# A Mamba scan on one Trainium2 core: C rows for five GpSimd products instead of three, brought by broadcast transfers

## The reference, cut to what matters

```python
h = relu(adj @ layernorm(x) @ gcn_w + gcn_b); h = layernorm(h) * ln_g + ln_b
xc, z = split(h @ w_in); u = silu(causal_conv4(xc))
dbc = u @ w_xp
dt = softplus(dbc[:, :8] @ w_dt + b_dt)
B, C = dbc[:, 8:24], dbc[:, 24:40]
hst = exp(dt*A) * hst + dt*B*u          # a recurrence over the 8192 tokens, for each channel and state
y = (sum over the 16 states of hst * C) + u * D_skip
x = x + (y * silu(z)) @ w_out
```

## Time and profile before

| | us |
|---|---|
| median of three runs | 1697.73 (1697.00 to 1698.45) |
| the profiled execution | 1698.79 |
| its span, first to last instruction | 1696.9 |
| steps 4 to 15, from ScalarE's copy at the head of step 4 to that of step 16 | 294.43 to 1246.9 |

### The profile page before, as it was taken

One profiled execution on the slowest core, in us unless ns is written; L12 is line 12 of the kernel. 1 busy time (PEld: TensorE's weight loads), 2 busy tenths in 40 slices (PEclk: granted clock), 3 DMA queues, 4 the chain that ended last, 5 costly groups with the idle time before them and its releaser, 6 DMA issues. The chain is left out here.

```text
span 1696.9 us, 21136 instructions
## 1 busy us (share of the span) xinstructions
PE 1556.1 (92%) x5282; PEld 791.8 (47%) x5282; DVE 1482.2 (87%) x1687; ACT 1005.5 (59%) x2093; POOL 1041.3 (61%) x471
## 2 busy tenths in 40 slices
PE   6999999999999999999999999999977677999994
PEld 2444344444444434343444444444422225999993
DVE  8416999999999999999999999999996995557998
ACT  2244666667575757576666667575757554555552
POOL 4024788887878778878788787878885651001221
PEclk9999999999999999999999999999988899999997
DMA  8976665757566666665665757566610202000002
GB/s 311 343 253 236 229 213 196 255 169 272 197 241 224 215 242 205 235 214 213 224 229 187 257 171 269 203 237 230 209 47 0 94 6 106 0 0 1 0 0 99
DMA packets 52073, 298.31 MB, mean 176 GB/s; under 512 B 5522, under 2 KB 5522, under 8 KB 19092
## 3 DMA queue, kind: packets, MB, share of 16 engines
q1 hardware_dynamic: 49680, 293.30, 48.8%
q10 hardware_dynamic: 2308, 4.20, 0.6%
HBM read 285.68 MB, written 11.80 MB: 175 GB/s over the span
## 5 line engine op out<-in xcount | busy, mean ns | idle before, releaser
L509 PE MATMUL bank<-ring,xh 128*128 128x512 f32 x2048 | 953.1, 593 | 15.5 <-DVE xh L989 15.0
L890 POOL TENSOR_TENSOR work<-work 128x1024 f32<-128x1024 f32 x210 | 516.6, 2460 | 238.3 <-DVE work L1081 232.0
L1123 DVE TENSOR_TENSOR_SCAN work<-bank,hstate,work 128x512 f32<-128x512 f32 x512 | 627.2, 1266 | 2.7 <-ACT bank L760 1.3
L509 PEld LDWEIGHTS bank<-ring,xh 128*128 128x128 f32 x2048 | 388.4, 190 | 458.3 <-issue 422.3
L760 ACT ACTIVATE bank<-work,a_neg 128x512 f32<-128x512 f32 x512 | 345.6, 688 | 306.2 <-DVE work L1123 305.9
L1073 DVE TENSOR_TENSOR work<-work,bank 128x1024 f32<-128x1024 f32 x256 | 309.5, 1214 | 60.0 <-PE bank L446 46.3
L446 PE MATMUL bank<-bc_parts,sel 96*128 96x512 bf16 x512 | 192.9, 385 | 33.3 <-DVE work L1081 25.8
L1081 DVE TENSOR_TENSOR work<-work,bank 128x1024 f32<-128x1024 f32 x182 | 216.2, 1194 | 0.0
L441 PE MATMUL bank<-work,w_sb 128*128 128x512 f32 (+2 forms) x352 | 183.5, 618 | 25.4 <-ACT work L676 11.2
L951 POOL TENSOR_TENSOR work<-work 128x256 f32 x32 | 28.5, 891 | 235.9 <-ACT work L797 235.9
L853 POOL TENSOR_TENSOR work<-work 128x1024 f32<-128x1024 f32 x48 | 113.3, 2361 | 79.9 <-ACT work L658 79.7
(11 more groups left out here) (148 smaller groups left out, 1581.4 us busy)
## 6 DMA issues: line engine op xcount, KB each, us to landing
ring<-adj_t SPq DMA_DIRECT2D x256, 1024.0 KB, 4.8
xh<-x_rows SPq DMA_DIRECT2D x16, 256.0 KB, 6.7
work<-x_t SPq DMA_DIRECT2D x16, 256.0 KB, 4.8
x_scratch<-work ACTq DMA_DIRECT2D x16, 256.0 KB, 5.4
work<-x_scratch SPq DMA_DIRECT2D x1, 4096.0 KB, 13.6
out_t<-work SPq DMA_DIRECT2D x16, 256.0 KB, 2.7
xl_scratch<-work SPq DMA_DIRECT2D x13, 256.0 KB, 2.2
ring<-xl_scratch SPq DMA_DIRECT2D x1, 3328.0 KB, 13.1
```

The costliest lines, as they stand in the source:

```text
L509: last = nc.tensor.matmul(mixed[:, :], xn[:, j, :], a, start=(j == 0), stop=(j == BLK - 1))
L890: nc.gpsimd.tensor_tensor(out=acc, in0=hc[0] if n == 1 else acc, in1=hc[n % 2], op=ALU.add).then_inc(y_added, 1)
L1123: nc.vector.tensor_tensor_scan(hb[s % 2][:, h, :], da[h], dbu[s % 2][:, h, :], hstate[:, HV * s + h:HV * s + h + 1], ALU.mult, ALU.add).th ...
```

## The change

`POOL_HC` becomes (1, 3, 8, 10, 14). For these five states TensorE's spread of the C row and ScalarE's copy are left out in all steps but the draining ones. Instead, in slot 9 of each step ScalarE stores rows 16 to 31 of `dbc` (the f32 values of C, 32 KB) to a new scratch tensor `c_dram`, and in the next step issues five loads (`load_c`), each of which reads one row of 512 values into all 128 partitions (256 KB), into one of two buffers: for states 1, 3, 8, 10 and 14 in slots 0, 2, 6, 8 and 12. The second buffer `c_two` takes the place of `bias_rows`, so the biases are now loaded at the start of step 16, after GpSimd's last product that reads a row there, and `fold_bias` moves behind slot 0 of that step. TensorE's waits for a free `c_bank` now count VectorE's products only.

```diff
-POOL_HC = (3, 8, 10)
+POOL_HC = (1, 3, 8, 10, 14)
+C_LOAD = {0: 1, 2: 3, 6: 8, 8: 10, 12: 14}
...
+def c_spreads(cs, n):
+
+    if isinstance(cs, int) and cs >= NC - 2:
+        return (DS - len(POOL_HC)) * (NC - 2) + DS * (cs - (NC - 2)) + n + 1
+    return hc_count(cs, n, False)
...
+    c_dram = nc.dram_tensor("c_scratch", (NC, DS, CH), F32, kind="Internal").ap()
...
-        bias_rows = sb("bias_rows", [2, 4 * D])
+        c_two = sb("c_two", [P, CH])
+        bias_rows = c_two[0:2, :]
...
-        c_one = carve(CH)
+        c_rows = [carve(CH), c_two[:, :]]
...
             def step(k, par, adj, pre, scan, post):
-                if isinstance(k, int) and k == NC:
-                    fold_bias()
...
                 def spread_c(n):
-                    if drains(k) and (cs > NC - 2 or n >= 1):
-                        pe.wait_ge(c_copied, hc_count(cs, n - 1, True))
-                    elif n >= 2 and n - 2 in POOL_HC:
-                        pe.wait_ge(c_copied, hc_count(cs, n - 2, True))
-                    else:
-                        wait_hc(pe, cs, n - 2)
+                    if drains(k):
+                        if cs == NC - 2 and n == 0:
+                            pe.wait_ge(hc_done, hc_count(cs - 1, DS - 1, False))
+                        else:
+                            pe.wait_ge(c_copied, DS * (cs - (NC - 2)) + n)
+                    elif n in POOL_HC:
+                        return
+                    elif n >= 2:
+                        wait(pe, hc_done, hc_count(cs, n - 2, False))
+                    elif not (isinstance(cs, int) and cs == 0):
+                        pe.wait_ge(hc_done, hc_count(cs - 1, DS + n - 2, False))
...
                 for s in range(16):
+                    if isinstance(k, int) and k == NC and s == 1:
+                        fold_bias()
...
-            act.dma_start(bias_rows[:, :], lstm_bias).then_inc(bias_loaded, 16)
...
+                if isinstance(k, int) and k == NC:
+                    act.wait_ge(pool_hc_done, len(POOL_HC) * (NC - 2))
+                    act.dma_start(bias_rows, lstm_bias).then_inc(bias_loaded, 16)
...
                     if s == 9:
                         written("dbc")
+                        wait(act, c_stored, 16 * (k - 1))
                         nc.scalar.activation(dbc[0:XPW, :], shared[0:XPW, :], ACT.Copy).then_inc(shared_read, 1)
                         act.wait_ge(shared_read, shared_index("dbc", k, pre, post) + 1)
+                        act.dma_start(c_dram[k - 1], dbc[DS:2 * DS, :]).then_inc(c_stored, 16)
...
+                def load_c(n):
+
+                    i = POOL_HC.index(n)
+                    b = (par + i) % 2
+                    act.wait_ge(c_stored, 16 * (cs + 1))
+                    wait(act, pool_hc_done, hc_count(cs, n, True) - 2)
+                    act.dma_start(c_rows[b], c_dram[cs, n:n + 1, :].broadcast_to([P, CH])).then_inc(c_row_in[b], 16)
...
                 for s in range(16):
-                    if scan and s >= 1 and (drains(k) or s - 1 in POOL_HC):
+                    if scan and drains(k) and s >= 1:
                         copy_c(s - 1)
...
+                    if scan and not drains(k) and s in C_LOAD:
+                        load_c(C_LOAD[s])
...
                 def make_hc(n):
-                    pool.wait_ge(c_copied, hc_count(cs, n, True))
+                    if drains(k):
+                        pool.wait_ge(c_copied, DS * (cs - (NC - 2)) + n + 1)
+                        c = c_sb[n % 2]
+                    else:
+                        i = POOL_HC.index(n)
+                        b = (par + i) % 2
+                        pool.wait_ge(c_row_in[b], 8 * (len(POOL_HC) * cs + (i - b)) + 16)
+                        c = c_rows[b]
...
                 def make_hc(n):
-                    dve.wait_ge(c_ready, DS * cs + n + 1)
+                    dve.wait_ge(c_ready, c_spreads(cs, n))
```

More of the change, by code:

```diff
@@ L265, in build @@
         xt_in = [sem(f"xt_in{i}") for i in range(2)]
+        c_row_in = [sem(f"c_row_in{i}") for i in range(2)]
+        c_stored = sem("c_stored")
         row_sum, row_mean, row_centred, row_sq = sems("row_sum row_mean row_centred row_sq")
@@ L394, in fold_bias @@
                 nc.tensor.matmul(mixed[:, :], less_first[:, :], W("w_ih"), start=True, stop=False)
-                nc.tensor.matmul(mixed[:, :], first_row[:, :], bias_rows[:, :], start=False, stop=True).then_inc(folded, 1)
+                nc.tensor.matmul(mixed[:, :], first_row[:, :], bias_rows, start=False, stop=True).then_inc(folded, 1)
             def step(k, par, adj, pre, scan, post):
-                if isinstance(k, int) and k == NC:
-                    fold_bias()
                 if isinstance(k, int) and k == 1:
@@ L727, in copy_c @@
                 def copy_c(n):
-                    act.wait_ge(c_ready, DS * cs + n + 1)
-                    if drains(k):
-                        act.wait_ge(adj_used, PIECES * NC)
-                        wait_hc(act, cs, n - 2)
-                        dest = c_sb[n % 2]
-                    else:
-                        wait(act, pool_hc_done, hc_count(cs, n, True) - 1)
-                        dest = c_one
-                    nc.scalar.activation(dest, c_bank[0 if drains(k) else n % 2][:, :], ACT.Copy).then_inc(c_copied, 1)
+                    act.wait_ge(c_ready, c_spreads(cs, n))
+                    act.wait_ge(adj_used, PIECES * NC)
+                    wait_hc(act, cs, n - 2)
+                    nc.scalar.activation(c_sb[n % 2], c_bank[0][:, :], ACT.Copy).then_inc(c_copied, 1)
+                def load_c(n):
[4 more added lines that the diff above has]
+                    act.dma_start(c_rows[b], c_dram[cs, n:n + 1, :].broadcast_to([P, CH])).then_inc(c_row_in[b], 16)
                 def save_state(c, n):
@@ L903, in make_hc @@
                         wait(pool, y_added, (DS - 1) * cs + (n - 1))
-                    c = c_sb[n % 2] if drains(k) else c_one
                     nc.gpsimd.tensor_tensor(out=hc[n % 2], in0=hb[n % 2], in1=c.unsqueeze(1).broadcast_to([P, HV, CH]),
```

## The result

The changed kernel takes 1754.35 us (median of 4 runs, 1752.59 to 1755.11) against 1698.09 for the kernel before beside it (4 runs). The ratio is 1.0325, 95% interval 1.0305 to 1.0345. The change was forecast slower by 1.3% and is slower by 3.3%, above the top of the range. The profiled execution took 1755.01 us, its span is 1753.1: 56.2 us more than before where I had summed 22.7.

The account below looks back on a forecast made before the run. Each step was bound by two legs: dtu to dbu 7 through adj piece 2 and TensorE, then to the next dtu through GpSimd. 19.6 - 1.5 + 4.6 = +22.7 us gave 1720.4 us; eight-in-ten range 1701 to 1730.

Parts of the forecast that it names:

- the bound: A loop step has two legs: dtu to dbu 7 through adj piece 2 and TensorE, then to the next dtu through GpSimd.
- the first half of the mechanism: Product 14 on GpSimd ahead of `make_xl` makes the xl store and adj piece 2 2.52 us later; TensorE waits.
- the term for twelve steps: Steps 4 to 15: xc1 and dbu 7 later by 1.29 us (five even steps) or 1.88 (seven others), +19.6 us.
- there are five pairs of adj products of 1.72: TensorE's work from piece 2 to xc1, with small products and xc0, priced at 10.12 us in all.
- Steps 2 and 3: No ring wait there; product 1 and c1, c3 shorten leg one: -1.5 us, between 0 and -2.2.
- Step 16: Start of step 16: biases load only after product 14 of step 15, first scan and y later: +4.6 us.
- its landing: The biases' load before the fold in step 16, taken as 2.2 us; with the long landing of 4.8, +7.2 us.
- dtu sets dbu 0: End of leg two: VectorE without product 14 is ready 1.12 us sooner but waits 1.12 longer for GpSimd's dtu; gain 0.
- 1693 by TensorE not being late: Rival: piece 2 has unseen slack, so GpSimd is the next limit in leg one; -4.7 us, 1693 us, chance 0.13.
- its next limit: In leg one, scan 3 may not overwrite what product 1 reads on GpSimd until 709.65; 0.26 us gained in odd steps.
- Row loads in the ring's way: Rival: a row load between adj pieces 2 and 3 makes TensorE 0.6 us later per step; 1728 us, chance 0.12 (1724 to 1731).
- As meant: Rival: VectorE sets the whole step and all 31 us come off; with +4.6, 1671 us, chance 0.02.

Follow-up runs that it names:

- The run with filled idle time: The changed kernel with 14 spare selector products on TensorE ahead of the wait for adj piece 2, steps 4 to 15: 1728.54 us, ratio 1.0175.
- the late `make_xl`: The kernel before, with only `make_xl` put behind add 15 on GpSimd, 2.3 us later, no row loads: 1730.81 us, ratio 1.019.
- `make_xl` first: The changed kernel with `make_xl` moved on GpSimd ahead of product 14, right after dtu: 1704.37 us, ratio 1.0044 to the kernel before.

## Why the prediction was right or wrong

**Right: the bound and the first half of the mechanism.** Product 14 delays `make_xl` by 2.5 us (4.83 after dtu's end, "4.9" forecast), the ring by as much, TensorE waits 3.8 us for piece 2 ("3 to 4"), VectorE waits at b4 and b6 as well as at b7, and gains nothing from the two products taken off it. The run with filled idle time gives the size that I had worked out: 18.5 us in eleven steps against 17.7. So do the six steps of the late `make_xl` in which the clock stays: 81.0 to 81.4 us, where I had 80.9 to 81.3.

**Wrong: the size of the term for twelve steps**, +19.6 against +46.4. The step that failed is in the part on TensorE: "there are five pairs of adj products of 1.72". I took that price from rows at 2.4 GHz and used it behind an idle time of 3 us which the change itself makes. Right there the granted clock is 0.52 and a pair costs up to twice as much. The filled run prices it: 23.1 us in the first eleven steps. The kernel before shows no such place in the loop, its idle times at piece 2 being 0.9 us and less; but elsewhere it has some (from 1247 to 1290 us, in step 16, the granted clock is 0.88), so that the clock can be lower where TensorE waits was to be read, and belonged into the range. I had listed the lower clock nowhere, not even as a rival.

**Steps 2 and 3:** -1.4 measured, -1.5 forecast.

**Step 16: +11.3 against +4.6.** The load was issued at 1251.8 on the old scale, 1252.0 forecast. But its landing, which I made the term, set nothing: the fold began at 1299.89, behind gcn, and that behind the copy of the adj sum (774), which waited 7.99 us in ScalarE's queue behind the load's wait. I named the folded weights and da 0 as what waits there, not this copy. The three products then ran at the lower clock (2.05, 1.92 and 2.07 us, where a pair of rows takes 1.12 in the earlier trace rows), so the folded weights came 2.4 us later than forecast. The y product behind costs 2.0 more: 3.92 us for 1.90. Before, VectorE began it 0.09 us ahead of GpSimd's product and GpSimd was the one held up:

```profile
1256.71 1.90 DVE L1049 TENSOR_TENSOR work<-work 128x1024 f32<-128x1024 f32 x1
```

```profile
1256.80 3.90 POOL L905 TENSOR_TENSOR work<-work,xh 128x1024 f32<-128x1024 f32 x1
```

Now GpSimd begins first (1308.12 against 1308.85), and it is VectorE. The Trainium skill, "SBUF — State Buffer", section "Who interferes with whom", says that order decides which of the two is held; the two traces agree. Together 2.4 + 2.0 = 4.4 of the 6.7 us that were missing. The last 2 us come behind dbu 2: 1.9 less up to the last scans, 4.0 more behind them at a clock of 0.76, in a place where a kernel without this change at step 16 loses the same.

**Half right: "dtu sets dbu 0".** In odd steps it does: in step 9 of the changed kernel VectorE waits 1.07 us for it (1.4 forecast). In even steps VectorE idles 2 us at the loop's jump, whenever dtu comes; that was 1.26 with product 14 still there. The gain of product 14 was 0 in both, for two reasons.

**The rivals.** 1693 by TensorE not being late did not happen. Where I made it happen, with `make_xl` first, its next limit (product 1 ahead of scan 3) was 0.27 us away and not reached; b7 was waited for as before, and scan 0 waited for product 14. Row loads in the ring's way: refuted for three loads a step, with which the loop takes what it took before; with five and `make_xl` first no step from 4 to 14 is longer than before, and there is no wait for the ring. GpSimd waits for no load, as forecast. As meant: no. The true case, slower through a falling clock, was not among them.

## What to carry to other kernels

Before an operation is added to an engine with room, follow what stands behind it on that engine to the queues that wait for it; here it was an unrelated transfer behind a store, and moving `make_xl` ahead of the new product takes away 50 of 56 us. If a forecast makes TensorE wait for some microseconds, price the products behind the wait at the lower clock too, as an upper bound, since not every wait is followed by it; in this kernel it more than doubled the loss in the loop. A load that is moved into an engine's order brings its wait along, for every instruction behind it.

## What the runs showed of the hardware

- TensorE idle for 2.7 to 3.6 us at piece 2 came back to a granted clock of about 0.5 in all twelve steps of the changed kernel (0.52 in step 8; 1.6 and 3.1 us more in steps 8 and 7). With 2.2 to 2.5 us, in the kernel with a late `make_xl`, it did in six steps of twelve, and one wait of 3.37 us in the kernel without product 1 on GpSimd left it at 1.00. Fourteen spare products in the gap kept it at 1.00 in all twelve.
- Products of VectorE and GpSimd that overlap hold each other up by order: 1.90 and 3.90 us when VectorE begins first, 3.92 and 2.90 when GpSimd does.
- VectorE is idle for 1.95 to 2.00 us where the loop jumps back, even with dtu there some 10 us earlier; with one product more in front of the jump it was 1.26.
- A C row of 2 KB read into 128 partitions lands in 4.4 and 4.8 us (the medians for the two buffers) beside the ring's traffic, and 36 of them lengthen the twelve steps by 0.7 us (953.1 for 952.4).
